# A graph-network kernel whose 64-wide edge features get a queue of their own, and whose summing matmuls all move 64 columns

## The reference

```python
# layer 0: h = relu(layernorm(x))
agg64  = segment_sum(edge_attr_64  @ W_edge.T, dst, 12500) / max(degree, 1)
x = x + concat(h @ W_self.T, agg64 @ W_neigh.T) @ W_final.T + b_final
# layer 1: h = relu(layernorm(x))
agg128 = segment_sum(edge_attr_128, dst, 12500)
x = x + relu(concat(h, agg128) @ W1 + b1) @ W2 + b2
```

## Time and profile before

| | |
|---|---|
| median of 3 runs | 527.18 us (526.82 to 532.25) |
| the profiled execution | 524.22 us |
| its span, from first to last instruction | 522.0 us |
| mean granted TensorE clock | 0.967 of full |
| PE, DVE, POOL, ACT busy | 490.3, 391.0, 343.7, 182.6 us |
| moved by DMA | 169.58 MB, mean 325 GB/s |

### The profile page before, as it was taken

The page is one execution under the profiler, slowest core; times in us unless marked ns, Lnnn a source line. Parts: engine busy times, 40 slices in busy tenths (PEclk is TensorE's granted clock), DMA queues, the critical chain, the costliest instruction groups (busy, mean ns, idle before and its releaser), DMA issues.

```text
span 522.0 us, 26395 instructions
## 1 busy us (share of the span) xinstructions
PE 490.3 (94%) x10865; PEld 438.7 (84%) x10865; DVE 391.0 (75%) x1416; ACT 182.6 (35%) x407; POOL 343.7 (66%) x528
## 2 busy tenths in 40 slices
PE   8999887899999999989999999999999999998995
PEld 8889777888988889878887888889888888887785
DVE  5548979779986789977887889989879988953002
ACT  0011124334634335442434344535433633432101
POOL 2787565767698555986759787797875775933200
PEclk9998989999999999999999999999999999999667
DMA  8999999999999999999999999999999999989201
GB/s 281 387 382 338 350 319 374 360 326 310 350 378 357 369 367 322 353 311 358 361 337 360 323 352 330 351 369 290 378 379 379 346 364 344 354 311 326 94 21 34
DMA packets 100945, 169.58 MB, mean 325 GB/s; under 512 B 11564, under 2 KB 65900, under 8 KB 100823
## 3 DMA queue, kind: packets, MB, share of 16 engines
q1 hardware_dynamic: 91923, 154.44, 84.5%
q10 hardware_dynamic: 8900, 13.43, 7.3%
HBM read 161.43 MB, written 6.40 MB: 321 GB/s over the span
## 4 chain that ended last, share of the span: by engine, by line
PE 66%; DVE 13%; issue 9%; POOL 4%; DMA 3%; DVEq 2%; SPq 1%; ACT 1%; ACTq 0%; POOLq 0%
PE ps L683 24%; PE ps L701 13%; PE ps L685 5%; PE ps L772 5%; PE ps L763 4%; PE ps L730 3%; PE ps L721 3%; PE ps L765 3%; PE ps L749 3%; DVE agg L1116 3%; DMA ring<-in_edge_attr_dram 3%; POOL hot_sum L569 2%; DVE onehot L1086 2%; POOL hot_part L569 2%; DVE merged L1208 1%
## 5 line engine op out<-in xcount | busy, mean ns | idle before, releaser
L685 PE MATMUL ps<-onehot,ring 128*64 128x50 f32 (+22 forms) x3126 | 215.3, 226 | 7.9 <-issue 7.7
L683 PEld LDWEIGHTS ps<-onehot,ring 128*64 128x64 f32 x3126 | 198.3, 141 | 28.5 <-issue 21.1
L683 PE MATMUL ps<-onehot,ring 128*64 128x50 f32 (+22 forms) x3126 | 215.0, 226 | 3.5 <-issue 2.6
L685 PEld LDWEIGHTS ps<-onehot,ring 128*64 128x64 f32 x3126 | 198.4, 141 | 8.8 <-issue 8.8
L569 POOL TENSOR_TENSOR hot_part<-onehot 128x240 bf16<-128x240 f32 (+26 forms) x128 | 94.6, 739 | 135.9 <-DVE onehot L1086 131.9
L1116 DVE TENSOR_TENSOR agg<-ps,agg 128x120 f32 (+22 forms) x319 | 85.2, 267 | 100.2 <-PE ps L710 77.0
L1086 DVE TENSOR_TENSOR onehot<-iota_win,rel 128x300 f32<-128x300 f32 (+29 forms) x192 | 136.7, 712 | 0.1
L701 PE MATMUL ps<-onehot,ring 128*64 128x50 f32 (+22 forms) x3126 | 121.8, 225 | 7.4 <-issue 7.4
L701 PEld LDWEIGHTS ps<-onehot,ring 128*64 128x64 f32 x3126 | 109.4, 141 | 8.3 <-issue 8.1
L569 POOL TENSOR_TENSOR hot_sum<-hot_part 128x100 bf16<-128x100 bf16 (+22 forms) x96 | 43.7, 455 | 7.5
L931 ACT ACTIVATE hn<-x,nmr,rstd 128x128 f32<-128x128 f32 x98 | 40.4, 482 | 21.3 <-DVE nmr L1183 21.2
(11 more groups left out here) (131 smaller groups left out, 668.0 us busy)
## 6 DMA issues: line engine op xcount, KB each, us to landing
ring<-in_edge_attr_dram SPq DMA_DIRECT2D x190, 192.0 KB, 4.6
ring<-in_edge_attr_dram SPq DMA_DIRECT2D x32, 832.0 KB, 5.6
ring<-in_edge_attr_dram SPq DMA_DIRECT2D x64, 384.0 KB, 4.5
ring<-in_edge_attr_dram SPq DMA_DIRECT2D x96, 256.0 KB, 4.5
ring<-in_edge_attr_dram SPq DMA_DIRECT2D x32, 416.0 KB, 7.7
ring<-in_edge_attr_dram SPq DMA_DIRECT2D x96, 128.0 KB, 4.9
ring<-in_edge_attr_dram SPq DMA_DIRECT2D x126, 96.0 KB, 4.2
x<-in_x_dram ACTq DMA_DIRECT2D x23, 256.0 KB, 6.0
```

The costliest lines, as they stand in the source:

```text
L683: nc.tensor.matmul(bank[0:H, o:o + w], ring128[0:K, slot, u, 0:H], hots, start=u == 0, stop=r == R - 1, skip_group_check=True)
L685: nc.tensor.matmul(bank[H:P, o:o + w], ring128[0:K, slot, u, H:D], hots, start=u == 0, stop=r == R - 1, skip_group_check=True)
```

## The change

From tick 7 on (`ON_ACT`, the tick behind chunk 127's), the 64-wide features are loaded by ACT, at the start of its tick t for chunk t+3, and a chunk's batches go in one DMA of three dimensions. SP keeps the 128-wide ones. The slot's semaphore rises by 16 for each DMA of SP and by 16 for ACT's one. PE's matmuls on the features move all `WIN` = 64 columns whatever the chunk's width, and the results lie 64 columns apart in the bank. The degrees' matmuls, POOL's sums and DVE's adds keep the chunk's width. DVE's one-hots keep it too, but for ticks 0 to 3, whose four buffers are filled to 64 columns so that nothing undefined is read. At ticks 5 to 8 PE runs three fillers each.

```diff
@@ build_gnn @@
+    ON_ACT = AT[CH - 1] + 1
...
-        in_slot[t % SLOTS] += 32 * (3 if c == CH - 1 else PARTS[c // 32])
+        in_slot[t % SLOTS] += 96 if c == CH - 1 else PARTS[c // 32] * 32 if t < ON_ACT else PARTS[c // 32] * 16 + 16
@@ SP load_edges @@
                 for ring, feats in ((ring128, edge_attr_128), (ring64, edge_attr_64)):
+                    if ring is ring64 and t >= ON_ACT:
+                        continue
@@ PE sums @@
-                bank, w = ps[:, t % BANKS, :], width_of(c)
+                bank, w, n = ps[:, t % BANKS, :], WIN, width_of(c)
...
                 for u, h, i, K in single:
-                    nc.tensor.matmul(bank[h * H:h * H + H, places[i][h]:places[i][h] + w], ones_h[0:K, :], halves[0:K, u, 0:w, 1],
+                    nc.tensor.matmul(bank[h * H:h * H + H, places[i][h]:places[i][h] + n], ones_h[0:K, :], halves[0:K, u, 0:n, 1],
@@ PE ticks @@
                 if t < 5:
                     keep_busy(BANK_TP, 4)
+                elif t < 9:
+                    pe.wait_ge(s_wsb, 3)
+                    keep_busy(BANK_HID, 3)
@@ ACT @@
+            def load_edges(t):
+                c = ORDER[t]
+                slot, e0, R, nb = t % SLOTS, first_edge(c), run_of(c), PARTS[c // 32]
+                act.wait_ge(s_mm, t - SLOTS + 1)
+                act.dma_start(ring64[:, slot, 0:nb * R, :].rearrange("p (b r) f -> p b (r f)", b=nb),
+                              edge_attr_64[e0:e0 + nb * R * P, :].rearrange("(b p r) f -> p b (r f)", p=P, r=R)).then_inc(s_load[slot], 16)
             def inputs(t):
+                if ON_ACT <= t + 3 < CH:
+                    load_edges(t + 3)
@@ DVE one_hots @@
-                a, b, w = n * part // parts, n * (part + 1) // parts, width_of(c)
+                a, b, w = n * part // parts, n * (part + 1) // parts, width_of(c) if t >= HOTS else WIN
@@ DVE adds @@
-                    nc.vector.tensor_tensor(here, ps[:, t % BANKS, o:o + n * w].rearrange("p (a n) -> p a n", a=n), here,
+                    nc.vector.tensor_tensor(here, ps[:, t % BANKS, o:o + n * WIN].rearrange("p (a n) -> p a n", a=n)[:, :, 0:w], here,
                                             ALU.add).then_inc(s_added, 1)
-                    o += n * w
+                    o += n * WIN
```

More of the change, by code:

```diff
@@ L104, in build_gnn @@
     AT = {c: t for t, c in enumerate(ORDER)}
+    ON_ACT = AT[CH - 1] + 1
+    assert ON_ACT >= SLOTS
     SECOND = 1 + -(-(N - FIRST_W) // GW)
@@ L258, in build_gnn @@
     HOTS = 4
+    assert all(ORDER[t] < 32 for t in range(HOTS)), "the first one-hots in each buffer fill all its units"
     AHEAD = 3
@@ L709, in sums @@
                 for k, (h, i, K) in enumerate(sums_of_hots):
-                    last = nc.tensor.matmul(bank[h * H:h * H + H, places[i][h]:places[i][h] + w], ones_h[0:K, :], hot_sum[0:K, hot, k, 0:w],
+                    last = nc.tensor.matmul(bank[h * H:h * H + H, places[i][h]:places[i][h] + n], ones_h[0:K, :], hot_sum[0:K, hot, k, 0:n],
                                             start=False, stop=True, skip_group_check=True)
@@ L1111, in adds @@
                     planes = (slice(0, 2), slice(0, 3, 2), slice(0, 3))[kind]
-                    n, w = 3 if kind == 2 else 2, width_of(c)
+                    n = 3 if kind == 2 else 2
+                    w = width_of(c)
                     if ADDED[t] + i:
```

## The result

The changed kernel's median is 523.45 us of 19 executions, beside 529.03 us for the kernel before in as many on the same chips: a ratio of 0.988, with a 95% interval of 0.984 to 0.992, so 6.3 us or 1.2% less; the two medians lie 5.6 us apart. The forecast was 7.7 us less. Two of the changed kernel's 19 executions took 1150.69 and 2562.70 us, at a granted clock of 1.00, and nothing on record tells why; the others of both kernels scatter by 1 to 2% around the medians. The profiled one of the changed kernel is among its longer ones, 527.79 us.

A forecast was written before the change was run, and what follows sets the result against it. PE was taken to bound the kernel, losing time to half clock, instruction stalls and waits for ACT's copy. Terms -10.3 - 1.7 + 3.3 + 1.0 = -7.7 us took 527.2 to 519.5 us, range 506 to 535.

The forecast's parts named there:

- The clock at the end: PE from 480.9 us on: 64-column matmuls lift the half clock under narrow chunks, -10.3 us (gain 0 to 12.0).
- Columns: PE's feature matmuls: moving 64 columns hardly changes a record's time, +1.0 us (0 to 9.4).
- Fillers: PE, ticks 5 to 8: the added matmuls cost +3.3 us (0 to 3.3) and save -1.7 us of half clock.
- they can keep the clock up at 40.6: PE near the start: fillers prevent the 3.4 us at half clock from 40.6 us, so -1.7 us.
- ACT's issue, its waits and the start: ACT's 121 DMAs at 0.5 us each hide in its waits; loads and wider first one-hots don't delay PE: 0.
- Instruction fetches: PE's issue stalls inside chunks, some 18 us: two data queues might move them either way, 0 (-18 to +18).
- fetches get later: Rival, chance 0.20: the busier second queue delays PE's 87 instruction fetches from tick 7 on, 0.2 us each, 536.9 us.
- The clock isn't lifted: Rival, chance 0.13: PE's gaps, not its columns, decide the clock, so the end stays as it is, 529.8 us.
- Fetches get earlier: Rival, chance 0.15: most of PE's 18 us of issue stalls go, say 12, giving 507.5 us.
- Theories A and B: Changed kernel's repeat: A, queue and fillers' costs add up, 0.993; B, the queue costs only without fillers, 0.988.

The follow-up runs named there:

- the repeat's: The changed kernel run once more, unaltered, on the chip of the other repeats: ratio 0.990 to the kernel before, 519.78 us beside 526.22.
- the repeat without fillers: The changed kernel without PE's fillers at ticks 5 to 8, run again on a second chip: ratio 0.987 to the kernel before, 523.09 us.

## Why the prediction was right, and which steps were not

The sign, the mechanism and the size hold: 519.5 us was forecast and 523.45 measured, on chips where the kernel before took 529.03 and not 527.2; the difference of the two, -7.7, against -6.3. But the sum is right with luck in its terms: the clock gave more than its upper bound, and what the forecast had at 1.0 and 0 took most of the surplus.

- *The clock at the end, -10.3.* Right in mechanism, shown by both width-only kernels (0.979, 0.982; dense chunks alone 0.980) and by the kernel with the queue alone, where a fully busy PE stays at 0.67. The size was read from one execution. Its clock cost was 522.0 x (1 - 0.967) = 17.2 us, near the least of the 39 executions of before (16.7 to 25.7, mean 21.0). The mean fell by 15.5 us with the width, 12.5 with the dense chunks alone, both above the 12.0 that the prediction had as the upper end; at the same time the rest grew by 5.2 and 1.2 us. I carried the 3 us between profile and median over as a constant; a good part of it was half clock that the change takes away.
- *Columns, +1.0 (0 to 9.4).* In the time as a whole right: width everywhere against width in the dense chunks is 513.9 - 512.9 = +1.0 us in the mean span. In the table it parts into 4.0 more rest and 3.0 less clock cost, the first well beyond its uncertainty, the second just, with five executions on one side. So the price on PE was under-sized, and the clock paid for most of it. PE's busy time less the clock's cost says the same: 472.2 to 473.1 us in the three profiles with narrow matmuls ahead of the dense chunks (before, queue alone, dense chunks alone), 475.4 to 476.9 in the five with width everywhere, all loads and no fillers. Where on PE it falls is open, since the records of the middle stretch show little of it. From 180 to 420 us, L683 takes 103.5 us for 1536 records before (67.4 ns), L689 takes 105.0 for 1547 in the width-only kernel (67.9 ns); L701 57.6 and L707 57.5 us for 1536 each:

The groups of PE from 180 to 420 us, before and then width alone (times run, busy us, mean ns, idle before):

```profile
L683 PE MATMUL ps<-onehot,ring 128*64 128x54 f32 (+11 forms) x1536 | 103.5, 226 | 0.9 <-issue 0.9
L701 PE MATMUL ps<-onehot,ring 128*64 128x54 f32 (+11 forms) x1536 | 57.6, 225 | 2.9 <-issue 2.8
```

```profile
L689 PE MATMUL ps<-onehot,ring 128*64 128x64 f32 x1547 | 105.0, 224 | 0.9 <-issue 0.8
L707 PE MATMUL ps<-onehot,ring 128*64 128x64 f32 x1536 | 57.5, 222 | 1.5 <-issue 1.3
```

- *Fillers, +3.3 and -1.7.* The price was about right (+2.6 in the rest, without the queue; in the profiles the fillers' line takes 14.1 to 14.8 us in place of 10.3 to 10.4, so 4 us where 3.3 was the upper end), the return wrong: the clock's cost is 6.3 with them and 5.5 without, so nothing. The step that failed is "they can keep the clock up at 40.6": in the changed profile the last of them starts at 40.8 us, and the clock is at half from 42.0 to 52.2 all the same. Beside the queue, the fillers cost nothing measurable (518.9 and 520.4 us in span).
- *ACT's issue, its waits and the start, 0.* Right: 0.37 us an issue, no wait of PE for ACT of a microsecond, and none for a load.
- *Instruction fetches, 0 (-18 to +18).* This is the term that was mis-sized. Stalls rose from 18.1 to 26.4 us in the two profiles (22.0 in the repeat's; 23.1 and 25.2 with the width alone, so single profiles don't tell the queue's part), and the second queue costs +9.3 us by itself with narrow matmuls (6.5 with width, 1.6 with width and fillers, by the spans of the table). The rival "fetches get later" was thus the right mechanism, at 0.02 us (1.6 / 87) to 0.11 us (9.3 / 87) a fetch: 87 x 0.1 = 8.7 us was named as the point from which it cancels the gain, and in the changed kernel it took less than the width gave. Of the 9.3 us, 3.5 are more half clock. The Trainium skill, "DMA: Bandwidth & Descriptors" (queues, rings and completion order), has each DMA engine go round the queues with work; the runs agree with it in sign, 1.014 for the queue alone.
- *The other rivals.* "The clock isn't lifted" is refuted by the windows above: in the queue-only kernel there is no gap and half clock, in the width-only one the columns alone differ and the clock is full. "Fetches get earlier" is refuted too. What would really bring it is less data, not another queue.

So the terms came out, in mean span: width -10.3, fillers +3.4, queue +1.6, in sum -5.3; forecast, -9.3 for width (-10.3 and +1.0), +1.6 for the fillers, 0 for the queue, -7.7. The parting of the last two goes by the order: with the queue first it is +6.5 for the queue and -1.5 for the fillers. Over all executions with a clock on record, the two long ones aside, the three are -11.3, +2.7 and +2.8.

Two things stay open. Why queue and fillers don't add up (3.4 and 6.5 us alone on top of width, 5.0 together) isn't settled. Theories A and B of the repeats' expectations are not told apart for certain: the 0.987 of the repeat without fillers is nearer to A, but over all of its twelve executions it is 0.991, and that and the equal ratios of the changed kernel and of width and fillers are nearer to B. The intervals are half a per cent either way. And the stalls of single profiles (20 to 29 us in the eleven profiles with the width and all loads) scatter too much to put the queue's price at one place; that the stalls come of data traffic is shown for its amount, by the run without the 64-wide loads. For its split over two queues, packets that start 0.15 us later in four profiles against four speak for it, but that these 0.15 us make up the queue's price is only argued.

## What to carry to other kernels

Where the clock falls although PE is busy, look at how many columns its matmuls move: where a float32 record's pace hardly depends on them (here 67.4 and 67.9 ns), moving columns whose results nobody reads costs little and can bring the clock back, and it need only be done where the chunks are narrow. Take each part of such a change by itself: here width alone gives 0.979 to 0.982, the whole 0.988 to 0.990. A queue that already waits for the consumer gains nothing from a second one, and PE's instructions come by the same DMA engines as the data; and where a state of the clock makes the scatter, take its cost as a mean over executions, not from the one with the profile.

## What the runs showed of the hardware that I had not expected

- Leaving out 48 of 168 MB of data took PE's instruction stalls from 23 to 1.7 us, and the kernel from 0.979 to 0.950, although PE waited for the data itself only once in width alone, for 0.3 us.
- One stall of 2.05 us near the start was followed by 10.2 us at half clock with matmuls on PE throughout, and 14 us in the kernel with width in the dense chunks alone (0.52). In the profile of before, the stretches there were 3.4 us long. I have no cause for the length.
- The executions of one kernel differ much in what half clock costs them, and that is a good part of its scatter: 16.7 to 25.7 us in the 39 of the table for before, and to 34.4 in all 55 with a clock on record.
- PE's long stalls stand at fixed places of its program, 126 to 127 matmul records or a multiple apart, and end 1.0 to 1.9 us behind the end of an instruction packet (134 of 146).
- A second data queue cost 1.4% by itself, with the same bytes, while the first queue waited for a free slot and PE for no load.
